# A four-layer graph network on one core: gathers without a bound, an extra table row for empty places, and the mean row awaited late

## The reference, cut to what matters

```
h = max(layernorm(x), 0);  x = x + gnn_l(h, adj)      for l = 0, 1, 2, 3

gnn_0: mask = adj > 0
       agg  = mask @ h / max(sum(mask, 1), 1)
       relu(concat(h @ W_self + b_self, agg @ W_nb + b_nb) @ W_comb + b_comb)
gnn_1, gnn_2, gnn_3 (8, 4 and 1 heads), per head:
       Wh   = h @ W
       e    = leaky_relu(f_src[:, None] + f_dst[None, :], 0.2)   # f = Wh . a
       attn = softmax(where(adj > 0, e, -9e15), axis=-1)
       attn @ Wh                                                 # gnn_2: elu of it
```

## Time and profile before

| | |
|---|---|
| median of 3 runs | 1249.79 us (1248.19 to 1251.66) |
| the profiled execution | 1243.5 us, of which the span is 1241.8 us |
| TensorE (PE) busy | 897.9 us, 72% |
| VectorE (DVE) busy | 874.3 us, 70% |
| GpSimd (POOL) busy | 689.2 us, 56% |
| ScalarE (ACT) busy | 394.1 us, 32% |
| DMA | 242.74 MB in the span |

### The profile page before, as it was taken

The page is one execution under the profiler, slowest core; times in us unless marked ns, Lnnn a source line. Parts: engine busy times, 40 slices in busy tenths (PEclk is TensorE's granted clock), DMA queues, the critical chain, the costliest instruction groups (busy, mean ns, idle before and its releaser), DMA issues.

```text
span 1241.8 us, 12157 instructions
## 1 busy us (share of the span) xinstructions
PE 897.9 (72%) x2804; PEld 485.2 (39%) x2804; DVE 874.3 (70%) x2811; ACT 394.1 (32%) x1200; POOL 689.2 (56%) x648
## 2 busy tenths in 40 slices
PE   3985969999256476755999999477888834738674
PEld 1332434444044365542656666234444332313231
DVE  3867699930187698836999897088999945746563
ACT  3552656632023133321323333134354430101110
POOL 4043423365477777617777710377777007777772
PEclk9997989999679689896999999878888966968988
DMA  9999868722678688726757720366677116646662
GB/s 361 387 346 366 316 251 328 224 72 76 200 234 248 181 271 263 238 95 185 202 162 206 209 80 35 95 175 177 188 212 211 53 52 175 171 139 182 181 184 86
DMA packets 81447, 242.74 MB, mean 195 GB/s; under 512 B 16931, under 2 KB 19395, under 8 KB 77275
## 3 DMA queue, kind: packets, MB, share of 16 engines
q0 software_dynamic: 47488, 144.09, 40.1%
q1 hardware_dynamic: 33882, 97.82, 21.4%
HBM read 203.00 MB, written 53.64 MB: 207 GB/s over the span
## 4 chain that ended last, share of the span: by engine, by line
PE 29%; DVE 25%; POOL 16%; DMA 13%; issue 11%; ACT 5%; POOLq 1%; SPq 0%; ACTq 0%
POOL arena L1081 12%; PE psum L679 9%; PE psum L703 7%; PE psum L638 7%; DVE arena L1380 4%; DVE arena L1313 4%; DMA arena<-XV,arena 4%; DVE arena L1192 2%; ACT arena L795 2%; DMA arena<-T,arena 2%; DMA arena<-in_adj 2%; DMA arena<-in_L_gnn_a 2%; DVE arena L1130 2%; DVE arena L1282 2%; PE psum L749 1%
## 5 line engine op out<-in xcount | busy, mean ns | idle before, releaser
L1081 POOL DMA_INDIRECT arena<-T,arena x476 | 518.9, 1090 | 332.9 <-issue 180.3
L703 PE MATMUL psum<-arena,misc 128*128 128x512 f32 x426 | 229.1, 659 | 62.8 <-DVE arena L1380 46.6
L679 PE MATMUL psum<-arena 128*128 128x264 f32 (+1 forms) x832 | 221.1, 412 | 47.3 <-ACT arena L795 47.3
L638 PE MATMUL psum<-arena 128*128 128x512 f32 (+1 forms) x416 | 200.3, 624 | 28.8 <-ACT arena L808 16.4
L679 PEld LDWEIGHTS psum<-arena 128*128 128x128 f32 (+1 forms) x832 | 163.3, 201 | 122.6 <-ACT arena L795 72.3
L616 PE MATMUL psum<-misc,arena 128*128 128x128 f32 (+1 forms) x520 | 87.9, 295 | 145.7 <-ACT arena L779 78.3
L1380 DVE TENSOR_TENSOR arena<-arena 128x512 f32<-128x512 f32 x238 | 160.6, 686 | 1.8
L616 PEld LDWEIGHTS psum<-misc,arena 128*128 128x128 f32 (+1 forms) x520 | 65.4, 152 | 195.8 <-ACT arena L779 89.6
L703 PEld LDWEIGHTS psum<-arena,misc 128*128 128x128 f32 x426 | 82.1, 209 | 146.8 <-issue 100.2
L779 ACT ACTIVATE arena<-arena 128x512 f32<-128x512 f32 x104 | 84.4, 811 | 155.2 <-DVE arena L1289 146.5
L749 PE MATMUL psum<-arena 128*128 128x512 f32 (+1 forms) x208 | 113.2, 695 | 17.9 <-ACT arena L792 17.9
(11 more groups left out here) (138 smaller groups left out, 1006.6 us busy)
## 6 DMA issues: line engine op xcount, KB each, us to landing
arena<-in_adj SPq DMA_DIRECT2D x25, 1663.5 KB, 8.5
T<-arena SPq DMA_DIRECT2D x75, 260.0 KB, 3.6
arena<-T,arena POOLq DMA_INDIRECT x476, 3.8
T<-arena SPq DMA_DIRECT2D x25, 256.0 KB, 2.6
XV<-arena SPq DMA_DIRECT2D x25, 256.0 KB, 2.3
PW<-arena POOLq DMA_DIRECT2D x5, 1024.0 KB, 8.3
arena<-in_x SPq DMA_DIRECT2D x1, 3072.0 KB, 17.6
XV<-arena SPq DMA_DIRECT2D x1, 3072.0 KB, 23.0
```

Source lines behind the costliest of these rows:

```text
L638: last = e.matmul(p_own[which][0:n, :], HT[t % 2][:, k, 0:n], W0[which][:, k, :], start=k == 0, stop=k == 3 and which == 0)
L679: last = e.matmul(p_wh[0:n, a, :], ht[:, k, 0:n], WL[l][:, k, a, :], start=k == 0, stop=k == 3)
L703: e.matmul(p_num[s % 3].rearrange("p (a o) -> p a o", a=2), ident, halves(GB[:, BASE[l, s] + of[n][0], :])[:, :, 0:HALF], start=n == 0, st ...
L1081: e.indirect_dma_start(GB[:, BASE[l, s] + k, 0:ROW], None, dr["T"][l], bass.IndirectOffsetOnAxis(ap=(IDP if l else IDX)[:, t, k:k + 1], ax ...
```

## The change

**Places.** An unused place now carries the index N+1, and every table gets a row N+1: zeros with the score -1e30 in layers 1 to 3 (`LOW`), zeros with the place N+1 in layer 0. So every gather reads 128 rows. The bound is gone from the gathers; the scatter of the lists, the `XV` gather and the output scatter keep theirs. The clearing of the ring goes, and the mask `NEGM` goes from `shifted`. The four new rows and three mean rows' first contents are stored by seven small DMAs on SP, ahead of the loop over tiles.

**Mean row.** POOL waits for `mean_out` only ahead of tile 25's gather, the last of a layer. That only this tile can use the mean row is made sure by sorting on the true degree (0 for a node without neighbours, where it was 1) and by one more test for the flag (`LONE`).

```diff
+        for l, p in enumerate((32, 64, 64, 96)):
+            e.dma_start(dr["T"][l][N + 1:N + 2, :], mrow[p:p + 1, :]).then_inc(S["empty_row"], 16)
+            if l:
+                e.dma_start(dr["T"][l][N:N + 1, :], mrow[0:1, :]).then_inc(S["zero"], 16)
...
-        iota(ROWID, [[0, 1]], 1, 1)
...
+        memset(mrow[32:33, D:ROW], float(N + 1))
+        memset(mrow[64:65, HALF:HALF + 8], LOW)
+        memset(mrow[96:97, D:ROW], LOW)
...
-        e.memset(flat[:, 0:CLEAR], 0.0).then_inc(S["cleared"], 1)
...
-        e.memset(flat[:, CLEAR:], 0.0).then_inc(S["cleared"], 1)
...
                 e.indirect_dma_start(GB[:, BASE[l, s] + k, 0:ROW], None, dr["T"][l],
-                                     bass.IndirectOffsetOnAxis(ap=(IDP if l else IDX)[:, t, k:k + 1], axis=0),
-                                     bounds_check=N, oob_is_err=False).then_inc(S[f"gather{s % 8}"], 16)
+                                     bass.IndirectOffsetOnAxis(ap=(IDP if l else IDX)[:, t, k:k + 1], axis=0)).then_inc(S[f"gather{s % 8}"], 16)
...
-            e.wait_ge(S["mean_out"], 16 * (l if l < 3 else 4))
...
             for s in range(NT + lag):
+                if ORDER[s:s + 1] == [NT - 1]:
+                    e.wait_ge(S["mean_out"], 16 * (l if l < 3 else 4))
...
-            scan_step(e.tensor_scalar(deg, FOUND[:, t:t + 1], 1.0, None, ALU.max))
...
-        place(e.tensor_scalar(FARM, lists, 0.0, FAR, ALU.is_equal, ALU.mult))
+        place(e.tensor_scalar(EMPTY, lists, 0.0, float(N + 2), ALU.is_equal, ALU.mult))
...
-        place(e.tensor_scalar(NEGM, FARM, -2.5e26, None, ALU.mult))
+        place(e.tensor_scalar(LONE, LR[:, 0:NT - 1, 0], float(N + 1), None, ALU.is_equal))
...
-                e.tensor_tensor(IDP[:, t, 0:SLOTS[t]], GB[:, base:base + SLOTS[t], D], FARM[:, t, 0:SLOTS[t]], ALU.max).then_inc(S["moved"], 1)
+                e.tensor_copy(IDP[:, t, 0:SLOTS[t]], GB[:, base:base + SLOTS[t], D]).then_inc(S["moved"], 1)
...
-            yield
-            soft.wait()
-            soft(e.tensor_tensor(u, u, NEGM[:, t, 0:n].unsqueeze(2).broadcast_to([P, n, NH]), ALU.add))
```

More of the change, by code:

```diff
@@ L26 @@
 WIDE = 2 * HALF + 16
-FAR = 4096.0
+LOW = -1e30
 GUESS = float(0x5F3759DF - (1 << 30) - (1 << 22))
@@ L363, in edges @@
     IDX, IDP, NID = take(NT * NK, by_tile(NK), U32), take(NT * NK, by_tile(NK), U32), take(NT, None, U32)
-    FARM, NEGM, SHARE = (take(NT * NK, by_tile(NK)) for _ in range(3))
+    EMPTY, SHARE = (take(NT * NK, by_tile(NK)) for _ in range(2))
     SM = take(2 * NT * 8, ("p (a t h) -> p a t h", dict(a=2, h=8)))
-    FOUND, COUNT, DEG, RDEG, CAP = take(NT), take(NT), take(NT), take(NT), take(NT)
+    COUNT, DEG, RDEG, CAP = take(NT), take(NT), take(NT), take(NT)
     HS = take(4 * NT, ("p (k t) -> p k t", dict(k=4)))
@@ L370, in edges @@
     NCL = NK + 1
-    CLASS, ROWID = take(NCL), take(1)
+    CLASS = take(NCL)
     KIND, AHEAD, ONES = take(NCL * NT), take(NCL * NT + 1), take(NCL * NT)
@@ L378, in edges @@
     RS, NM, HV, TT = take(NT), take(NT), take(NT), take(NT)
-    hsum, mrow, fl = take(4), take(ROW), take(4)
+    hsum, mrow, fl, LONE = take(4), take(ROW), take(5), take(NT - 1)
     small = [take(20) for _ in range(2)]
@@ L391, in edges @@
     S1, S2, PA, PB = (take(4 * D, ("p (k o) -> p k o", dict(k=4))) for _ in range(4))
-    CLEAR = at[0] - ring
     MARK = [take(NSEG * PART // 2, None, FP16) for _ in range(2)]
@@ L428, in edges @@
     STEP_OF_LAST = ORDER.index(NT - 1)
-    SETUP = dict(ident=2, xpad=3, mark=7, eight=8, start=9, rowid=10, id=12, upper=14, mrow=16, ones=17, we=18, ones16=19, classes=20, line=21,
-                 sm=22, cap=22 + len(set(SLOTS)))
+    SETUP = dict(ident=2, xpad=3, mark=7, eight=8, start=9, id=11, upper=13, mrow=18, ones=19, we=20, ones16=21, classes=22, line=23,
+                 sm=24, cap=24 + len(set(SLOTS)))
     def bank(kind, which, k):
@@ L718, in tensor @@
         e.wait_ge(S["fl"], 1)
-        e.matmul(p_small[:, 0:1], g["ones"], fl[:, 3:4], start=True, stop=True).then_inc(S["flag_mm"], 1)
+        e.matmul(p_small[:, 0:1], g["ones"], fl[:, 4:5], start=True, stop=True).then_inc(S["flag_mm"], 1)
         mean(0)
@@ L890, in mean_row @@
             else:
-                e.wait_ge(S["zero"], 16)
+                e.wait_ge(S["zero"], 4 * 16)
             for a in range(2):
@@ L1051, in gpsimd @@
         score_weights(3, 1)
-        e.wait_ge(S["reduced"], 6)
-        e.wait_ge(S["pw4"], 16)
-        e.wait_ge(S["scored"], 6)
-        flat = GB.rearrange("p n o -> p (n o)")
-        e.memset(flat[:, 0:CLEAR], 0.0).then_inc(S["cleared"], 1)
-        e.wait_ge(S["cleared"], 1)
         e.wait_ge(S["mark"], NT - 2)
         e.memset(ADJ[(NT - 1) % 2][96:P, :], 0.0).then_inc(S["adjpad"], 1)
-        e.wait_ge(S["adjpad"], 1)
-        e.wait_ge(S["scan"], NT)
-        e.memset(flat[:, CLEAR:], 0.0).then_inc(S["cleared"], 1)
         e.wait_ge(S["ranked"], 1)
@@ L1081, in rows_of @@
                 e.indirect_dma_start(GB[:, BASE[l, s] + k, 0:ROW], None, dr["T"][l],
-                                     bass.IndirectOffsetOnAxis(ap=(IDP if l else IDX)[:, t, k:k + 1], axis=0),
-                                     bounds_check=N, oob_is_err=False).then_inc(S[f"gather{s % 8}"], 16)
-        e.wait_ge(S["cleared"], 2)
+                                     bass.IndirectOffsetOnAxis(ap=(IDP if l else IDX)[:, t, k:k + 1], axis=0)).then_inc(S[f"gather{s % 8}"], 16)
+        e.wait_ge(S["scan"], NT)
+        e.wait_ge(S["reduced"], 6)
+        e.wait_ge(S["pw4"], 16)
+        e.wait_ge(S["scored"], 6)
         wait_pieces(e, "tout", NT - 1, NT)
@@ L1088, in gpsimd @@
         e.wait_ge(S["x_kept"], 16 * 5)
-        e.wait_ge(S["zero"], 16)
+        e.wait_ge(S["zero"], 4 * 16)
+        e.wait_ge(S["empty_row"], 4 * 16)
         e.wait_ge(S["places"], 32)
@@ L1197, in vector @@
                 reduce(*REDUCES[t])
-            r, deg = R[:, t, 0:NK], R[:, t, NK:NK + 1]
+            r, found = R[:, t, 0:NK], R[:, t, NK:NK + 1]
             pick, column = (v.rearrange("p (s k) -> p s k", k=8) for v in (PICK, COLUMN))
@@ L1259, in vector @@
         place.wait()
-        e.scalar_tensor_tensor(IDX, lists, -1.0, FARM, ALU.add, ALU.add).then_inc(S["idx"], 1)
+        e.scalar_tensor_tensor(IDX, lists, -1.0, EMPTY, ALU.add, ALU.add).then_inc(S["idx"], 1)
         place(e.reciprocal(RDEG, DEG))
@@ L1271, in vector @@
         place(e.tensor_reduce(fl[:, 2:3], CAP, AX.X, ALU.max))
+        place(e.tensor_reduce(fl[:, 3:4], LONE, AX.X, ALU.max))
         place.wait()
-        e.tensor_reduce(fl[:, 3:4], fl[:, 0:3], AX.X, ALU.max).then_inc(S["fl"], 1)
+        e.tensor_reduce(fl[:, 4:5], fl[:, 0:4], AX.X, ALU.max).then_inc(S["fl"], 1)
         ln, added, soft, blend = (Steps(e, S[n]) for n in ("ln_step", "added", "soft_step", "blended"))
@@ L1487, in program @@
         dr["LIST"] = scratch("LIST", [NT * P, LROW])
-        dr["T"] = [scratch(f"T{l}", [N + 1, ROW]) for l in range(4)]
+        dr["T"] = [scratch(f"T{l}", [N + 2, ROW]) for l in range(4)]
         words = 51160
```

9 lines of the change are left out of this document (3 added, 6 removed).

## The result

The changed kernel takes 1234.8 us (median of 4 runs, 1229.7 to 1236.1), the one before 1249.0 us beside it (1246.0 to 1251.7). The ratio is 0.989, 95% interval 0.987 to 0.991: faster, by 14 us where 42 were forecast. The profiled execution took 1235.2 us.

The account below looks back on a forecast made before the run. The prediction took POOL's gathers, issued without pause at 1.31 us each, to set the end in layer 3, TensorE in layer 1, VectorE in layer 2. Terms 11.9 + 3 - 1 + 28.8 = 42.7 us off 1249.8 gave 1208; range 1160 to 1241.

Parts of the forecast that it names:

- mean row awaited late: Starts of layers 1 to 3: first gathers no longer wait for the mean row, 3.1, 2.9 and 5.9 us, 11.9 gained.
- mask gone: VectorE: 78 additions fewer, worth it only where VectorE sets the pace, mainly layer 2; 3 us gained.
- empty places fetched: Gathers: about 1,860 more rows a layer on DMA engines with room, a tile's last gather landing later; 1 us lost.
- the bound gone: POOL's gathers: 0.10 us less each without the index comparison, 28.8 us gained over the four layers; the disputed term.
- list stage: Before layer 0's gathers: ring clearing and seven small DMAs count 0 us; the stage's end at 316 us should not move.
- The rival of the repeated row: Last gathers of each tile, above all the 15-slot one: repeats slow, 110 us lost, 1317 to 1346; chance 0.10 with alignment.
- mild form: Milder repeated-row case: 1254 to 1275 us; 0.5 us more per gather of repeats, 15 us in all, begins to decide.
- The estimate of 1238 by that half rate: Gathers of repeats at half rate take 1 us more each, 30 us in all, so a time near 1238.
- The bound is free: Rival on POOL's gathers: duration stays 1.00 us and gap 0.30, only 13.9 us gained, 1236; chance 0.30.
- The ring's place: Rival: removed buffers shift the ring by 417 words, changing row alignment; no cost given, counted within the slower case's 0.10.
- The 13.0 us that the prediction names for layer 3's boundary: Layer 3's start: first gathers begin 13.0 us after the first of SP's last stores, expected to become some 7.
- the two memsets of the ring: List stage: clearing the ring no more gains 0 us, as the memsets had more than 20 us of cover.

Follow-up runs that it names:

- g2: The changed kernel with a layer's first gather waiting for the mean row again; 1247.3 us, ratio to the kernel before 1.000.
- g1: The changed kernel with the bound (N+1) back on the gathers, the same rows fetched; 1246.5 us.
- e9: The changed kernel with layer 3's mean row stored in one piece, and bound, index beyond it and mask back for tiles 24 and 0 alone; 1222.6 us.
- e11: The changed kernel with layer 3's mean row in one piece, small stores later on SP, and a separate empty row for each partition; 1221.3 us.
- g3: The changed kernel with 128 empty rows per table, tiles 24 and 0 skipping again, one-piece mean row, later small stores; 1227.8 us, ratio 0.986.

## Why the prediction was wrong

Its terms (us gained; measured by the stages above, undoing one thing each):

```text
term                      forecast   measured
mean row awaited late       11.9      10.6 (g2)
mask gone                    3        open (m)
empty places fetched        -1        -(13.5 + m), from g1 against before
the bound gone              28.8      12.7 (g1)
list stage                   0        -2.9
sum                         42.7       6.9 (spans of the two traces; 7 to 14 by the runs)
```

The third line is a difference: g1 is the kernel before with the late wait, the fetch and without the mask, and takes 2.9 us more after the list stage, though the late wait gives 10.6. It assumes that the terms add, and is good to some 3 us. By layer the 13.5 are 5.0, 4.3, 4.0 and 0.3. Skipping or spreading the rows gave back 8.7 and 8.6, nearly all in layers 1 and 2; what the 5 us of layer 0 are is open.

**The bound, half the size.** The failed step, and the largest in us, is "I take 0.10 us, nearer to zero because comparing is the lightest of the three". The bound takes 0.05. The measured value lies inside the bounds of 0 and 0.76, and it was right that the gap of 0.30 doesn't belong to it. What a saved microsecond is worth was nearly right as well: 28.8 of 47.6 offered was forecast (0.61), 12.7 of 23.8 came (0.53). By layer, half the forecast would be 4.2, 1.8, 2.5 and 6.0; measured were 6.0, 3.3, 0 and 3.9.

**The empty places, the step that failed most in kind.** "A tile's last gather ... now lands later by a part of its 3.7 us; once per layer", -1 us in all. I looked at mean DMA shares of 60 to 64% and saw room. The volume was near: POOL's queue moves 158.86 MB and moved 144.09, 14.8 MB more, with 15.5 forecast. But the empty places are not spread evenly: e9, which skips those of tiles 24 and 0 alone, moves 151.45 MB, so half of them are in two of the 26 tiles. Tile 0's 15 gathers follow each other at 1.26 us, and VectorE waits for the last of them. It was used 2.1 us after its start because nearly all of it was skipped, a row that I had not looked at. Now it takes 6 to 9 us.

**The rival of the repeated row** named that place, and e11 shows its mechanism: with distinct rows 3.5 to 4.5 us, with one row 6 to 9. Its price was far too high (110 us, and 15 in the mild form just to decide; for the 1254 to 1275 of that form the text gives no sum); e9 and e11 got 8.7 and 8.6 us back, the one-piece row included. I treated it as a case beside the gains, with one chance in ten, where it was a cost that comes with them. "Tile 25's gather lands in 4.1 us where others take 3.7" was weak evidence, one gather whose like was not in flight beside it. The Trainium skill ("DMA: Bandwidth & Descriptors", Latency and other measured facts) has copies at half rate when all partitions' streams have a row pitch of 4 MiB, and infers that they meet in one memory channel. The direction agrees with 7.0 against 4.5 us here; that the cause is a channel no run shows. The estimate of 1238 by that half rate is near the measured time too, but by luck: it adds 30 us for the repeats to a sum with 28.8 for the bound, and both are more than twice what was measured.

**The bound is free** gave 1236, near the 1234.8, and was wrong in cause, so its nearness is luck: the bound is worth 12.7 us, and the fetch took as much.

**The ring's place** shows no cost on the engines: VectorE's steps over the fetched rows take 684 ns (L1375, before L1380) and 744 ns (L1311, before L1313: 743), as before. Whether rows land more slowly at the new alignment was not tested apart.

**The late wait** was right: 11.9 forecast, 10.6 measured. The 13.0 us that the prediction names for layer 3's boundary count from one store earlier than the other two. In layer 3 the first gather starts 2.4 us behind SP's store, not 7.8; the first landing is 3.2 us later through the mean row's own store, which I had not priced, and it hardly matters, as POOL sets the pace there.

**The list stage** grew by 2.9 us in both traces of the changed kernel, where I had said it should not move. It grows while the adjacency matrix is scanned: VectorE starts on the last tile (L1193) at 251.7 us, before at 249.0, in e11 at 243.2 and in g3 at 253.2, and from there to the first gather it takes 74.6 to 75.9 us in every kernel of the table. So the two memsets of the ring were indeed worth nothing. The seven small DMAs start the third adjacency tile's load 1.2 us later (14.0 us for 12.8), but g1 has the same 14 and a list stage of 323.9. Kernels whose list stage differs little take 318.1 to 328.5 us. The cause stays open, and it is as large as most terms here.

**Two slips of the sum.** 1249.8 - 42.7 is 1207.1, which doesn't round to 1208, and half of 6.4 is 3.2 and not the 3.5 taken for layer 1. Neither changes anything.

## What to carry to other kernels

When skipped work is replaced by harmless work, look where it is concentrated and who waits for the last piece of it, not at the mean share of the engine that does it; here, padding that all points to one row was slower to fetch than the same number of distinct rows. A later start of the issuing engine was paid in full here (g2), a later first landing hardly. A late landing in mid-layer was paid for in layers 1 and 2 and not in layers 0 and 3 (e9), so look at what sets the pace behind it before giving it a price. Before trusting a term of some us, compare stages that the edit does not touch: here one of them moved by as much.
